# The second attention's scores in three head groups and its values as one 512-wide operand; rows first in the first attention

## The reference, cut to what matters

```
x = x + L0_xattn(layernorm(x), ctx)         # 16 heads of 16
x = x + L0_ffn(layernorm(x))                # quantised gate, up, down
x = x + L1_xattn(layernorm(x), ctx, mask)   # 16 heads of 64, a null key, layer norms before and after
x = x + L1_ffn(layernorm(x))                # 8 experts, the best 2 weighted
```

```
x = layer_norm(x, g_norm);  q = x @ Wq;  k, v = split(context @ Wkv)
k, v = concatenate([null, k]), concatenate([null, v])
attn = softmax(where(mask, q k^T * scale, max_neg))
out = layer_norm((attn @ v) @ Wout, g_out)
```

## Time and profile before

| | us |
|---|---|
| median of 3 runs (1131.32 to 1134.66) | 1132.56 |
| the profiled execution, its own time | 1126.59 |
| its span, first to last instruction | 1124.9 |
| PE busy | 1045.4 (93%) |
| DVE busy | 940.4 (84%) |
| ACT (ScalarE) busy | 698.8 (62%) |
| POOL (GpSimd) busy | 482.3 (43%) |
| mean granted TensorE clock | 0.962 |

### The profile page before, as it was taken

How to read it: one execution, slowest core, us unless ns; L and a number is a source line. 1 busy time by engine, 2 the same in 40 slices (tenths; PEclk the granted TensorE clock), 3 DMA queues, 4 the chain that set the end, 5 groups by cost and what they waited for, 6 DMA issues and landing times.

```text
span 1124.9 us, 21027 instructions
## 1 busy us (share of the span) xinstructions
PE 1045.4 (93%) x6538; PEld 887.2 (79%) x6538; DVE 940.4 (84%) x2536; ACT 698.8 (62%) x1831; POOL 482.3 (43%) x543
## 2 busy tenths in 40 slices
PE   7999999998799879787898999999999889999997
PEld 5877787887588656443798999999999877777786
DVE  6798998887776799899566899999998778888885
ACT  2666767765455889577876678778777423333333
POOL 2344445342000578675001356666665434433343
PEclk8999999999899999788798999999999989999999
DMA  9000000000224486699301411011100000000000
GB/s 287 8 2 2 1 1 1 1 2 1 109 116 161 159 284 247 236 356 320 93 1 52 122 50 47 2 48 48 48 1 2 1 1 29 19 19 19 19 19 29
DMA packets 50648, 83.31 MB, mean 74 GB/s; under 512 B 4716, under 2 KB 36288, under 8 KB 50560
## 3 DMA queue, kind: packets, MB, share of 16 engines
q1 hardware_dynamic: 49183, 81.43, 21.2%
q10 hardware_dynamic: 1376, 0.79, 0.3%
HBM read 45.98 MB, written 36.23 MB: 73 GB/s over the span
## 4 chain that ended last, share of the span: by engine, by line
PE 43%; DVE 5%; issue 1%; ACT 1%; DMA 1%; POOL 1%; DVEq 0%; POOLq 0%; ACTq 0%
PE m_ps L2438 13%; PE a_ps L1325 10%; PE a_ps L1268 10%; PE f_ps L2339 5%; PE a_ps L1283 3%; PE m_ps L2466 1%; DMA k_raw<-vw_scratch 1%; PE m_ps L2486 1%; PE a_ps L1302 1%; DVE m_xl L2636 1%; PE m_ps L2475 0%; DVE m_ls L2599 0%; DVE m_g L2623 0%; DVE m_sel L2612 0%; DVE a_mx L1467 0%
## 5 line engine op out<-in xcount | busy, mean ns | idle before, releaser
L1348 ACT ACTIVATE a_U<-a_ps,a_mx 128x80 f32<-128x80 f32 x512 | 125.7, 330 | 27.8 <-DVE a_mx L1467 24.9
L1410 POOL TENSOR_TENSOR a_xrs<-a_xve,mhalf 128x1 f32<-128x1 f32 x32 | 31.7, 989 | 154.6 <-DVE a_xve L1528 154.6
L2543 POOL TENSOR_TENSOR m_half<-m_half 128x512 f32<-128x512 f32 x32 | 41.0, 1282 | 130.0 <-ACT m_half L2503 130.0
L1417 POOL TENSOR_TENSOR a_U<-a_U,a_rc 128x1280 f32<-128x1280 f32 x32 | 74.7, 2334 | 33.7 <-DVE a_rc L1457 33.7
L2510 ACT ACTIVATE m_ex<-m_ls 128x8 f32<-128x8 f32 x32 | 6.7, 209 | 129.2 <-DVE m_ls L2599 129.2
L2438 PE MATMUL m_ps<-m_wh,m_xh 128*128 128x512 f32 x256 | 86.6, 419 | 0.0
L1075 DVE TENSOR_SCALAR a_U<-a_ps 128x320 f32<-128x320 f32 x128 | 59.2, 483 | 28.5 <-PE a_ps L868 20.6
L2186 POOL TENSOR_SCALAR f_sg<-f_sg 128x1024 f32<-128x1024 f32 x24 | 37.0, 1542 | 105.1 <-ACT f_sg L2075 104.6
L2438 PE MATMUL m_ps<-m_wh,m_xl 128*128 128x512 f32 x256 | 80.9, 397 | 0.0
L2438 PE MATMUL m_ps<-m_wl,m_xh 128*128 128x512 f32 x256 | 80.3, 394 | 0.0
L961 PEld LDWEIGHTS a_ps<-vals,a_PT 128*128 128x128 f32 x640 | 76.4, 192 | 2.0 <-issue 0.4
(11 more groups left out here) (270 smaller groups left out, 3329.3 us busy)
## 6 DMA issues: line engine op xcount, KB each, us to landing
up_scratch<-f_ub SPq DMA_DIRECT2D x24, 512.0 KB, 2.9
f_ul<-up_scratch SPq DMA_DIRECT2D x24, 512.0 KB, 5.5
key_scratch<-p_keys SPq DMA_DIRECT2D x8, 640.0 KB, 6.6
vw_scratch<-p_vw SPq DMA_DIRECT2D x16, 320.0 KB, 5.8
k_raw<-key_scratch SPq DMA_DIRECT2D x8, 640.0 KB, 5.4
k_raw<-vw_scratch SPq DMA_DIRECT2D x4, 1280.0 KB, 6.0
h_scratch<-f_hh SPq DMA_DIRECT2D x8, 512.0 KB, 2.7
h_scratch<-f_hl SPq DMA_DIRECT2D x8, 512.0 KB, 3.2
```

Source lines behind the costliest of these rows:

```text
L1348: last = act.activation(U[a.p][:, h * KP:(h + 1) * KP], bank(a, g)[:, (h % 4) * KP:(h % 4 + 1) * KP], ACT.Exp, bias=mx[a.p][:, h:h + 1])
L1417: pool.tensor_tensor(heads(U[a.p]), heads(U[a.p]), rc[a.p][:].unsqueeze(2).broadcast_to([P, H, KP]), ALU.mult).then_inc(s_N, 1)
```

## The change

In the second attention:

- Scores come in three groups, of 6, 6 and 4 heads (480, 480 and 320 columns), each with a bank of its own: group g is always in S[g], and waits for the exponentials of the same group of the tile before. There are 18 matmuls instead of 24, three maxima instead of four, and the 16 exponentials in three runs.
- High and low values lie side by side in one tile `VW` [128, 2, 10, 256]. Ten matmuls of 512 columns put `PTs` x high in the left half of Y and `PTs` x low in the right half; ten of 256 columns add `PTl` x high to the left half.
- The output is then in two halves. ScalarE copies the right half to `yb` (counted by `s_y2`), DVE adds the left half to it (new, counted by `s_y3`), and `s_y3` frees the bank and starts the statistics. The copy is now the first instruction of ScalarE's `body(t)`, the add the first of DVE's.

In the first attention PE's and ScalarE's bodies take the rows of tile t+3 before the first eight probability transposes and the first two casts.

```diff
-        vhigh0, vlow0 = self.place("VW_high0", [P, NJ, D], F32R), self.place("VW_low0", [P, NJ, D], F32R)
+        values0 = self.place("VW0", [P, 2, NJ, D], F32R)
...
-        vhigh1, vlow1 = self.place("VW_high1", [P, NJ, D], F32R), self.place("VW_low1", [P, NJ, D], F32R)
+        values1 = self.place("VW1", [P, 2, NJ, D], F32R)
...
-        self.vhigh, self.vlow = [vhigh0, vhigh1], [vlow0, vlow1]
+        self.values = [values0, values1]
+        self.vhigh, self.vlow = [[v[:, i, :, :] for v in self.values] for i in range(2)]
@@ -883,9 +884,6 @@
 
                 def body(t):
                     nxt, new, old = t + 2, t + 3, t + -1
-                    if t.ok():
-                        probs_T(t, 0)
-                        probs_T(t, 1)
                     if new.ok():
                         pe.wait_ge(s_xn, new.of(lambda n: n + 1))
                         if new.t0 >= 1:
@@ -898,6 +896,9 @@
                         last.then_inc(s_xT, 1)
                         if piece(t) is not None:
                             fw.transpose(pe, X, piece(t))
+                    if t.ok():
+                        probs_T(t, 0)
+                        probs_T(t, 1)
                     if nxt.ok():
                         pe.wait_ge(s_qe, nxt.of(lambda n: n + 1))
                         if nxt.t0 == 0:
@@ -985,11 +986,6 @@
                         act.wait_ge(s_PT, t.of(lambda n: 3 * n + k + 1))
                         act.copy(PTs[t.p][:, js[0]:js[-1] + 1, :].rearrange("p j n -> p (j n)"),
                                  R[k][:, 0:len(js) * P]).then_inc(s_PTe, 1)
-                    if t.ok():
-                        if t.t0 >= 2:
-                            act.wait_ge(s_PV, t.of(lambda n: n - 1))
-                        probs(0)
-                        probs(1)
                     if new.ok():
                         act.wait_ge(s_xT, new.of(lambda n: n + 1))
                         if piece(t) is not None:
@@ -997,8 +993,13 @@
                         if new.t0 >= 2:
                             act.wait_ge(s_q, new.of(lambda n: n - 1))
                         act.copy(xnT[new.p][:].rearrange("p k n -> p (k n)"), X[:, 0:D]).then_inc(s_xTe, 1)
-                        if piece(t) is not None:
-                            fw.high(act, X, piece(t))
+                    if t.ok():
+                        if t.t0 >= 2:
+                            act.wait_ge(s_PV, t.of(lambda n: n - 1))
+                        probs(0)
+                        probs(1)
+                    if new.ok() and piece(t) is not None:
+                        fw.high(act, X, piece(t))
                     if old.ok():
                         act.wait_ge(s_oT, old.of(lambda n: n + 1))
                     if t.ok():
...
+    GROUPS = [range(0, 6), range(6, 12), range(12, H)]
+    NG = len(GROUPS)
+
+    def columns(g):
+        return slice(GROUPS[g][0] * KP, (GROUPS[g][-1] + 1) * KP)
+
+    def width(g):
+        return len(GROUPS[g]) * KP
 
     with ExitStack() as st:
...
@@ -1256,8 +1262,8 @@
 
         def tensor(pe):
             def scores(a, g):
-                if 4 * a.t0 + g >= 3:
-                    pe.wait_ge(s_E, 4 * a.t0 + g - 2)
+                if a.t0 >= 1:
+                    pe.wait_ge(s_E, a.of(lambda n: NG * (n - 1) + g + 1))
...
                     for k in range(KT):
                         last = pe.matmul(
-                            bank(a, g)[:, 0:QW], x_[a.p][:, k, :],
-                            k_[a.batch % 2][:, k, g * QW:(g + 1) * QW],
+                            S[g][:, 0:width(g)], x_[a.p][:, k, :],
+                            k_[a.batch % 2][:, k, columns(g)],
@@ -1305,26 +1311,26 @@
                 if nxt.ok():
                     scores(nxt, 1)
                     scores(nxt, 2)
-                    scores(nxt, 3)
                 for n in weights_at(t)[0:3]:
                     if n == 0:
-                        pe.wait_ge(s_E, 4 * NT)
+                        pe.wait_ge(s_E, NG * NT)
                     mw.transpose(pe, S, n)
                 if t.ok():
                     if t.t0 % TPB == 0:
                         pe.wait_ge(s_vl, 4 * t.batch + 4)
                     if t.t0 >= 1:
-                        pe.wait_ge(s_y2, t.of(lambda n: n))
-                    vh, vl = fold.vhigh[t.batch % 2], fold.vlow[t.batch % 2]
-                    n = 0
-                    for p_, v_, ready in ((PTs, vh, s_PTe), (PTs, vl, None), (PTl, vh, s_PTl)):
-                        for k, js in enumerate(PTS):
-                            if ready is not None:
-                                pe.wait_ge(ready, t.of(lambda n: 3 * n + k + 1))
-                            for j in js:
-                                last = pe.matmul(Y[:, 0:D], p_[t.p][:, j, :], v_[:, j, :],
-                                                 start=(n == 0), stop=(n == 3 * NJ - 1))
-                                n += 1
+                        pe.wait_ge(s_y3, t.of(lambda n: n))
+                    v = fold.values[t.batch % 2]
+                    for k, js in enumerate(PTS):
+                        pe.wait_ge(s_PTe, t.of(lambda n: 3 * n + k + 1))
+                        for j in js:
+                            pe.matmul(Y[:].rearrange("p (i d) -> p i d", i=2), PTs[t.p][:, j, :], v[:, :, j, :],
+                                      start=(j == 0), stop=False, skip_group_check=True)
+                    for k, js in enumerate(PTS):
+                        pe.wait_ge(s_PTl, t.of(lambda n: 3 * n + k + 1))
+                        for j in js:
+                            last = pe.matmul(Y[:, 0:D], PTl[t.p][:, j, :], v[:, 0, j, :],
+                                             start=False, stop=(j == NJ - 1), skip_group_check=True)
                     last.then_inc(s_y, 1)
                 for n in weights_at(t)[3:6]:
                     mw.transpose(pe, S, n)
...
-                for h in range(4 * g, 4 * g + 4):
+                act.wait_ge(s_mx, a.of(lambda n: NG * n + g + 1))
+                for i, h in enumerate(GROUPS[g]):
                     last = act.activation(U[a.p][:, h * KP:(h + 1) * KP],
-                                          bank(a, g)[:, (h % 4) * KP:(h % 4 + 1) * KP], ACT.Exp,
+                                          S[g][:, i * KP:(i + 1) * KP], ACT.Exp,
                                           bias=mx[a.p][:, h:h + 1])
                 last.then_inc(s_E, 1)
 
             def body(t):
                 a, b, c_ = t + 2, t + 3, t + -1
+                if c_.ok():
+                    act.wait_ge(s_y, c_.of(lambda n: n + 1))
+                    if c_.t0 >= 2:
+                        act.wait_ge(s_x1, c_.of(lambda n: n - 1))
+                    act.copy(yb[c_.p][:], Y[:, D:2 * D]).then_inc(s_y2, 1)
                 if t.ok():
                     if t.t0 >= 2:
                         act.wait_ge(s_y, t.of(lambda n: n - 1))
@@ -1359,18 +1370,13 @@
                         probs(t, k)
                 if a.ok():
                     exps(a, 0)
-                if c_.ok():
-                    act.wait_ge(s_y, c_.of(lambda n: n + 1))
-                    if c_.t0 >= 2:
-                        act.wait_ge(s_x1, c_.of(lambda n: n - 1))
-                    act.copy(yb[c_.p][:], Y[:, 0:D]).then_inc(s_y2, 1)
                 if b.ok():
                     act.wait_ge(s_xT, b.of(lambda n: n + 1))
                     if b.t0 >= 2:
-                        act.wait_ge(s_S, b.of(lambda n: 4 * (n - 1)))
+                        act.wait_ge(s_S, b.of(lambda n: NG * (n - 1)))
                     act.copy(xnT[b.p][:].rearrange("p k n -> p (k n)"), X[:, 0:D]).then_inc(s_xTe, 1)
                 if a.ok():
...
@@ -1462,10 +1468,10 @@
                 def top(g):
                     if a.ok():
                         if g == 0 and a.t0 >= 2:
-                            dve.wait_ge(s_E, a.of(lambda n: 4 * n - 4))
-                        dve.wait_ge(s_S, a.of(lambda n: 4 * n + g + 1))
-                        dve.tensor_reduce(mx[a.p][:, 4 * g:4 * g + 4],
-                                          bank(a, g)[:, 0:QW].rearrange("p (h k) -> p h k", k=KP),
+                            dve.wait_ge(s_E, a.of(lambda n: NG * (n - 1)))
+                        dve.wait_ge(s_S, a.of(lambda n: NG * n + g + 1))
+                        dve.tensor_reduce(mx[a.p][:, GROUPS[g][0]:GROUPS[g][-1] + 1],
+                                          S[g][:, 0:width(g)].rearrange("p (h k) -> p h k", k=KP),
                                           AX.X, ALU.max, negate=True).then_inc(s_mx, 1)
 
                 def probs(k):
+                prev = t + -1
+                if prev.ok():
+                    dve.wait_ge(s_y2, prev.of(lambda n: n + 1))
+                    dve.tensor_tensor(yb[prev.p][:], Y[:, 0:D], yb[prev.p][:], ALU.add).then_inc(s_y3, 1)
                 top(0)
                 if (t + 1).ok():
                     sums(t + 1)
                 probs(2)
-                top(3)
```

(6 more changed lines are left out.)

13 lines of the change are left out of this document (5 added, 8 removed).

## The result

The changed kernel takes 1200.5 us, the median of 4 runs (1198.6 to 1202.0); the kernel before took 1131.9 us on the same chip. The ratio is 1.060, with a 95% interval of 1.056 to 1.064: 6% slower, where 1202 had been forecast. All of it stands in the second attention: from the last matmul of the feed-forward to the last update of `xs` there, the profile before has 282.2 us and the changed one 355.1, 72.9 more, where the spans differ by 72.0.

| | before | after |
|---|---|---|
| span, us | 1124.9 | 1196.9 |
| start of the output copy of tile 2, second attention | 657.84 | 658.40 |
| the same of tile 31 | 901.12 | 973.94 |
| between them | 243.3 | 315.5 |
| from there to the end (experts) | 223.8 | 223.0 |

The account below looks back on a forecast made before the run. The prediction took TensorE, busiest and at full clock, to bound both attentions. Terms +73.5 and -4 gave +69.5 us: 1196 from the profiled 1126.59, 1202 from the median 1132.56; range 1184 to 1224.

Parts of the forecast that it names:

- The ring: Second attention: DVE's body, GpSimd's work and ScalarE's copy wait in a circle, 11.2 us a tile against 8.39; +73.5 us.
- The last four tiles: End of the second attention: today's 33.7 us plus 1.5 for each tile, 39.7 us.
- First attention: Taking the rows earlier removes TensorE's waits for ScalarE's copy of them; -4 us, between -6 and +5.
- the bound of -6: First attention, best case: all of TensorE's waits for the copied rows are gone, -6 us.
- the +5 end: First attention, worst case: TensorE gets the normalised rows 0.16 us late in 32 tiles, +5 us.
- Fewer matmuls, three banks: Second attention: 16 fewer matmuls a tile, worth 3 us but covered, and one score bank a group; 0 us each.
- The 6.0 us that I put on top: Whole kernel: the median of the runs before lay 6.0 us above the profiled execution, raising 1196 to 1202.
- The ends of the range: Whole kernel: 10.7 to 11.8 us a tile in the second attention, with the first attention's ends; 1184 to 1224 us.
- ScalarE's idle before the copy: Sign in the second attention: some 3.5 us idle for GpSimd's xs update, nearly 30 times, about 90 us in all.
- The clock: Rival, second attention: pauses lower TensorE's clock, some 14 us a tile, about 1280 us; chance 0.07.
- A looser ring of 9.8 us: Rival, second attention: 1 us a tile gone in several places, 9.8 us a tile and 1165 us; chance 0.09.
- The "faster" rival: Rival, second attention: the copy finds its buffer free and TensorE stays the bound, 1126 us; chance 0.04.

Follow-up runs that it names:

- e1: The changed kernel with three output buffers yb instead of two, the copy's wait one tile looser; 1125.5 us, ratio 0.989 to the kernel before.
- e3: The changed kernel with one more 128x256 product on GpSimd, its result unread, ahead of the scaling of yb; 1217.2 us, ratio 1.071.
- e2: The changed kernel with GpSimd's work on yb and xs moved ahead of its two inverse roots, two buffers; 1164.2 us, ratio 1.022.
- e5: The kernel before with only the change's first attention (rows first); 1129.6 us, ratio 0.995.
- e6: The changed kernel with three output buffers yb and the old order of the first attention; 1132.6 us, ratio 0.997.
- e4: The kernel before with only ScalarE's output copy moved to the head of its body; four score groups, no add; 1175.2 us, ratio 1.034.
- e7: The changed kernel with 30 value products of 256 columns and no add on DVE; copy first, two buffers, three groups; 1136.7 us, ratio 1.002.
- e9: The same kernel as e1, the changed one with three output buffers, run again in another group; 1126.2 us, ratio 0.992.
- e8: The changed kernel with the copy back behind the first exponentials and DVE's add behind its second maximum, two buffers; 1163.3 us, ratio 1.025.

## Why the prediction was right

- **The ring**, term +73.5: +72.3 (315.5 - 243.3). Its parts came within a few hundredths: 7.51 us of DVE (7.5), 3.63 from variance to copy (3.64), 0.04 of semaphore (0.05); 11.17 and 10.67 the two periods (11.2 and 10.7). The last four tiles took 38.9 (973.94 - 935.03) where I had 39.7, by today's lengths and an extra of 1.5 each that was a guess. The copy of tile 2 stayed where it was, as said: it starts 30.3 us behind the last matmul of the feed-forward before the change and 30.5 with it.
- **That nothing could hide in it** is shown from three sides: a buffer more takes all of it away (e1), 0.56 us more on GpSimd are 0.56 us more in the period (e3), and 1.4 us less in the period (11.17 to 9.75) come from GpSimd's order alone (e2).
- **First attention**, term -4. By itself it is -5.3 (e5), and -5.9 in the traces up to tile 29, near the bound of -6. The wait of PE for ScalarE's rows is gone, and the +5 end, PE late for the normalised rows, did not come. (The output product of tile 29 starts 6.6 us earlier, at 265.29 against 271.90; 0.7 of these stand ahead of tile 0.) Of the rest of that profile, see the end.
- **Fewer matmuls, three banks**, 0 each: covered while the ring holds, as said. In e6, where nothing covers it, the second attention as a whole gives about 3 us, my figure for the matmuls; but the period goes from 8.39 to 8.35 only (over the same 25 tiles), 1.3 us up to the update of tile 24, the rest comes in the last seven tiles, and what part the banks have in it was not told apart. A bank for each group is worth much in another place: e4 and e7 have the same products and the copy in the same place, but four groups in three banks against three in three, and lose 38.9 and 13.5 us in the second attention. My expectation of e4 had overlooked it.
- **What was luck.** For the profiled execution the sum gives 1196, and it took 1198.6; for the median it gives 1202, and that is 1200.5. The 6.0 us that I put on top, because before the median lies so far above the profiled execution, are 1.9 here. The likely reason, not shown, is the fall of the clock told at the end: it stands in the changed profile and not in the one before. So part of the nearness of 1202 to 1200.5 is two errors of a few us that cancel. The ends of the range are also added up wrongly: 26 times -0.5 or +0.6 and the ends of the first attention give 1187 to 1227, not 1184 to 1224. The measured time lies in either.
- **Sizes that I had wrong.** ScalarE's idle before the copy is 4.4 us and 127.8 in all (page, part 5), not 3.5 and 90; DVE's before the add is 2.93, not 3.5: from the end of the variance to the next add it is 3.67, and DVE's split fills 0.74 of it. PE is busy 82% and not 74% (229.33 of 279): it pauses 2.07 us a tile where my 8.3 us of work in 11.2 left 2.9, since the same matmuls are recorded longer with pauses between them: the twenty value products take 4.28 us here (2.57 + 0.74 + 0.97), and 3.67 in e1, where they run without a pause. None of these is a term of the sum.
- **The rivals.** The clock did not fall in the second attention: 1.00 over 279 us with PE 82% busy and three pauses a tile of up to 0.91 us. So the rule of the Trainium skill (TensorE: Matmul & The Clock Gate, A second HAM failure mode: psum-queue depth-cycling), by which short pauses between groups make the clock go back and forth, did not decide here. A looser ring of 9.8 us is what e2 has, but only with another order. The "faster" rival needed the copy to find its buffer free; e1 gives it that, and its ratio is 0.989 (0.992 in e9), against 0.994 in the rival (1126 of 1132.6). I wrote that I saw no way to it by the queue order, and neither order tried reaches it (e2, e8); but one more buffer of 1 KB a partition was the way.

The best version found is the change with three buffers `yb`: 0.8 to 1.1% faster than the kernel before (0.8 from the larger number of runs), and by the ratios 6.4 to 6.7% faster than the change as made.

## What to carry to other kernels

Before an instruction goes to the head of an in-order engine's body, write down what it waits for, and follow that back until you come to the same engine or run out: if you come round, and the way is longer than the work of the busiest engine, the way sets the new period, however idle each engine on it looks. Then count by how many bodies the wait looks back, since that divides the sum. Here, with two buffers, the copy of body t waits for the update in GpSimd's body t-1, and every tile goes the whole way; with three it waits for that of body t-2, and the wait is gone. One more buffer can so turn a loss of 6% into a gain. My own list of rings was not complete (e4, e8), so look also for rings that go round over two tiles, and through the release of a bank. An edit that loses as a whole may be one missing buffer away from its gain, so take its parts one by one, and also together with the buffer.

## What had not been expected of the hardware

In the changed kernel's profile TensorE's granted clock falls at the end of the first attention, and gives back nearly all of the 5.9 us that rows first had won there. PE's output products of tiles 29, 30 and 31, timeline of the changed kernel:

```profile
265.29 1.13 PE L949 MATMUL a_ps<-wo,a_oT 128*128 128x256 f32 x4 [1.49 <-ACT a_oT L1010]
...
272.76 2.08 PE L949 MATMUL a_ps<-wo,a_oT 128*128 128x256 f32 x4 [0.74 <-ACT a_oT L1010]
...
281.59 2.07 PE L949 MATMUL a_ps<-wo,a_oT 128*128 128x256 f32 x4 [0.46 <-ACT a_oT L1010]
```

and the same of e3, with the same first attention:

```profile
271.95 1.13 PE L949 MATMUL a_ps<-wo,a_oT 128*128 128x256 f32 x4 [0.90 <-ACT a_oT L1010]
...
276.95 1.13 PE L949 MATMUL a_ps<-wo,a_oT 128*128 128x256 f32 x4 [0.46 <-ACT a_oT L1010]
```

Windows of 250:290, the changed kernel and then the kernel before (clock in the third column from the end; from 270 to 280 it is 0.50, the lower level, in the changed kernel and 1.00 before):

```profile
250.00:290.00 40.00, 30.62 (x171) 25.84 (x170) 25.16 (x79) 13.31 (x38) 8.56 (x13) 0.72 0.02 9
```

```profile
250.00:290.00 40.00, 30.28 (x216) 24.85 (x215) 30.52 (x97) 17.48 (x52) 11.84 (x19) 0.93 0.03 9
```

From tile 29 to tile 31 it takes 16.3 us with the fall and 10.5 without (in e3 tile 29 starts at 266.43): 5.8 us. The last tiles are where PE has long pauses of its own. The other profiles agree: 16.2 to 16.7 us in the nine profiles that have the fall, 10.5 in the three that have not. The fall comes with either order of the rows (with the old order in e4 and e6, and not in the kernel before; with rows first not in e3 and e7). So it differs between executions of the same first attention, and a profile with it and one without it differ by half a per cent for that reason alone; what decides it stays open, and whether the order of the rows makes it more frequent can't be told from twelve.

The other is the size of the contention between GpSimd and VectorE, told above under e2. The one that starts inside the other's time is the one that takes longer: GpSimd's root by 0.5 us and its update by 0.46, DVE's split of 640 columns by 0.42. GpSimd's scaling, which started first in e2, kept its 0.74.
